# A transformer block on one core: the products of P and V of a head pair in four groups instead of six

## The reference, cut to what matters

```python
# x: (2, 1024, 512) f32, 16 heads of d = 32
h = layernorm(x)
Q, K, V = (h @ Wq.T + bq), (h @ Wk.T + bk), (h @ Wv.T + bv)     # each cut into 16 heads
Q, K = rope(Q), rope(K)
scores = einsum('bhqd,bhkd->bhqk', Q, K) / sqrt(32)
attn = softmax(where(causal, scores, -inf), axis=-1)
x = x + einsum('bhqk,bhkd->bhqd', attn, V).reshape(...) @ Wo.T + bo
g, u = (layernorm(x) @ gate_w.T) * gate_s, (layernorm(x) @ up_w.T) * up_s
x = x + ((silu(g) * u) @ down_w.T) * down_s
```

## Time and profile before

| what | value |
|---|---|
| time, median of 3 runs | 858.93 us (858.11 to 862.7) |
| the profiled execution | 860.51 us, its span 858.5 us |
| PE busy | 779.1 us (91%) |
| DVE busy | 476.4 us (55%) |
| ACT busy | 329.0 us (38%) |
| POOL busy | 247.7 us (29%) |
| share of the chain that ended last | PE 66%, DVE 9%, DMA 8%, issue 8%, SP's queue 4%, ACT 3% |
| the products of P and V, L1106 | 768 records, 144.7 us busy |

### The profile page before, as it was taken

The page is one execution under the profiler, slowest core; times in us unless marked ns, Lnnn a source line. Parts: engine busy times, 40 slices in busy tenths (PEclk is TensorE's granted clock), DMA queues, the critical chain, the costliest instruction groups (busy, mean ns, idle before and its releaser), DMA issues.

```text
span 858.5 us, 10688 instructions
## 1 busy us (share of the span) xinstructions
PE 779.1 (91%) x3520; PEld 537.8 (63%) x3520; DVE 476.4 (55%) x1102; ACT 329.0 (38%) x669; POOL 247.7 (29%) x224
## 2 busy tenths in 40 slices
PE   4899999977999999999999999946999999999996
PEld 3678787744444445454444444735788888888885
DVE  5877596976667666767676744527412413314112
ACT  3423333424555555555555555210223223223221
POOL 0514152501113131313131315715122322323223
PEclk9989999967999999999999999986999999999999
DMA  8085634854556565656565626760000100100001
GB/s 269 29 325 192 220 122 172 262 181 126 137 138 163 138 164 139 163 138 162 138 162 139 163 65 196 269 286 1 1 0 1 50 1 0 49 1 24 27 0 51
DMA packets 52012, 104.37 MB, mean 122 GB/s; under 512 B 14820, under 2 KB 15332, under 8 KB 51444
## 3 DMA queue, kind: packets, MB, share of 16 engines
q1 hardware_dynamic: 51960, 103.72, 38.9%
HBM read 69.62 MB, written 38.21 MB: 126 GB/s over the span
## 4 chain that ended last, share of the span: by engine, by line
PE 66%; DVE 9%; DMA 8%; issue 8%; SPq 4%; ACT 3%; POOL 2%; DVEq 0%; ACTq 0%; POOLq 0%
PE ps L1002 31%; PE ps L1106 11%; PE ps L1180 9%; PE ps L1066 8%; PE ps L1087 5%; DMA flag_st<-in_ffn 5%; SPq L389 2%; DVE masked L855 2%; PE ps L994 2%; DMA qk_scratch<-st_lo 1%; DVE neg_max L873 1%; POOL xr L532 1%; ACT xT_hi L566 1%; DVE w_lo L768 1%; DVE rot L799 1%
## 5 line engine op out<-in xcount | busy, mean ns | idle before, releaser
L647 ACT ACTIVATE p<-ps 128x384 f32<-128x384 f32 (+3 forms) x384 | 171.9, 492 | 160.7 <-PE ps L1087 157.4
L1066 PE MATMUL ps<-k_st,q_st 96*128 96x512 f32 (+2 forms) x384 | 147.9, 411 | 21.8 <-DVE row_max L855 14.0
L855 DVE CUSTOM_DVE_ANT_0 masked<-ps,mask_qk 128x256 bf16<-128x256 f32 (+3 forms) x256 | 120.6, 500 | 66.5 <-PE ps L1066 65.8
L1106 PE MATMUL ps<-p,v_slot 128*64 128x512 f32 (+3 forms) x768 | 144.7, 500 | 1.2 <-ACT o_raw L654 1.2
L1066 PEld LDWEIGHTS ps<-k_st,q_st 96*128 96x128 f32 x384 | 72.6, 197 | 103.7 <-issue 51.9
L1087 PE MATMUL ps<-q_st,k_st 99*128 99x384 f32 (+2 forms) x384 | 131.3, 362 | 5.4 <-DMA q_st<-neg_max_T 4.0
L961 DVE SCALAR_TENSOR_TENSOR hid<-ps,us_sb,silu 128x512 f32<-128x512 f32 x44 | 33.0, 750 | 169.0 <-PE ps L1002 166.5
L516 POOL TENSOR_SCALAR_AFFINE_SELECT p<-p 128x512 f32<-128x512 f32 x64 | 41.0, 640 | 253.6 <-ACT p L647 253.6
L551 POOL TENSOR_TENSOR hid_lo<-hid,hid_hi 128x512 fp32r<-128x512 f32 x44 | 56.8, 1292 | 180.1 <-ACT hid_hi L722 180.1
L1106 PEld LDWEIGHTS ps<-p,v_slot 128*64 128x64 f32 x768 | 46.1, 136 | 66.9 <-issue 57.3
L857 DVE TENSOR_REDUCE row_max<-ps 128x1 f32<-128x512 f32 (+1 forms) x128 | 83.1, 651 | 4.4 <-PE ps L1066 2.0
(11 more groups left out here) (94 smaller groups left out, 1118.2 us busy)
## 6 DMA issues: line engine op xcount, KB each, us to landing
qk_scratch<-st_hi SPq DMA_DIRECT2D x32, 512.0 KB, 3.9
q_st<-qk_scratch SPq DMA_DIRECT2D x32, 384.0 KB, 4.2
k_st<-qk_scratch SPq DMA_DIRECT2D x32, 384.0 KB, 5.0
flag_st<-in_ffn SPq DMA_DIRECT2D x32, 264.0 KB, 2.8
ffn_copy<-in_ffn SPq DMA_DIRECT2D x32, 264.0 KB, 3.2
qk_scratch<-st_lo SPq DMA_DIRECT2D x16, 512.0 KB, 4.3
o_T<-o_raw SPq DMA_DIRECT2D x32, 128.0 KB, 2.6
rec_l<-rec_rows SPq DMA_DIRECT2D x32, 128.0 KB, 3.3
```

The costliest lines, as they stand in the source:

```text
L647: act.activation(p32[:, at:at + q0 + w - keep], ps[:, ST_BANK + i % RING, keep - q0:w], ACT.Exp, scale=SCALE).then_inc(exp_done, 1)
L855: ins = dve.tensor_tensor_reduce(masked[:, s_before(i) % 2, col:col + kept], scores, mask_qk[:, 512 - kept:512], 1.0, NEG, ALU.add, ALU.ma ...
L1066: ins = pe.matmul(ps[:, S_BANK + i % RING, col:col + w], q_st[0:K_DOT, slot, qt * P:(qt + 1) * P], k_st[0:K_DOT, slot, k0:k0 + w], start=T ...
L1106: ins = pe.matmul(ps[VW * a:VW * (a + 1), O_BANK + half, q0 - 512 * half:512], v_slot[:, slot, kt, :], p32[:, at:at + n], start=(kt == 0), ...
```

## The change

The pair's twelve (half, kt) are cut in four groups in place of six, and a step issues two groups, at its places 3 and 9, in place of three at 3, 7 and 11. The products themselves are the same.

```diff
-PV_AFTER = (3, 7, 11)
-PV_GROUPS = [[(0, 0), (0, 1)], [(0, 2), (0, 3), (1, 0)], [(1, 1), (1, 7)],
-             [(1, 2), (1, 6)], [(1, 3)], [(1, 4), (1, 5)]]
+PV_AFTER = (3, 9)
+PV_GROUPS = [[(0, 0), (0, 1), (0, 2), (0, 3)], [(1, 0), (1, 1)], [(1, 2), (1, 3), (1, 7)], [(1, 4), (1, 5), (1, 6)]]
...
                     if t >= 2 and i in PV_AFTER:
-                        output_products(t // 2 - 1, 3 * (t % 2) + PV_AFTER.index(i))
+                        output_products(t // 2 - 1, len(PV_AFTER) * (t % 2) + PV_AFTER.index(i))
```

## The result

The changed kernel takes 889.5 us in the median (four runs, 887.71 to 891.02), the kernel before 860.73 beside it (four runs, 858.11 to 862.7). The ratio is 1.0335, with an interval of 1.0295 to 1.0376: slower by 3.4%. The forecast was 871, with a range from 862 to 877. The sign was right, the size was not.

What follows compares the result with a forecast made beforehand. Bound: a loop from PE's transposition over SP's issues and the weights' piece to DVE's test. Steady part +9.4, steps 2 and 3 +0.9, 28 to 30 +0.1, t = 31 +1.6: +12.0 us, median about 871, range 862 to 877.

Steps and rivals of the forecast that it cites:

- The bound: Stage B's steady part: steps end on a loop through PE's transposition and DVE's test, not on PE's work alone.
- the loop: Stage B: PE's transposition, ACT's copy, SP's DMA issues, weights' piece, DVE's test, next step's first matmul; slack about 0.1 us.
- Longer group ahead of the transposition: Place 3 of each step: 384 more columns cost 0.64 us a step, with bounds 0.5 to 0.64.
- Fewer groups: Stage B: one group less a step gains nothing behind the transposition; 0.35 us a step if that cover were gone.
- POOL and the test: Odd steps: POOL's mask no longer lies over DVE's test, 0.33 us off each, bounds 0 and 0.33.
- Steps in which POOL scales: Four or five steps of B: the longer group hides under an existing wait; no loss, a gain of 0.1 at most.
- The end of B: Step t = 31: more products stand ahead of the last exponential, +1.6 us, bounds 0.6 to 1.9.
- Steps 28 to 30: Behind B's steady part: t = 28 costs 0; in 29 and 30 the saved 0.35 meets new waits; +0.1 us.
- The clock: Stage B: the sum adds nothing for a falling granted clock, as PE would idle only 1 us of 11.
- the third rival: Stage B: clock falls to 1.2 GHz in one step of ten, some 25 us on top, 896; chance 0.05.

Runs made afterwards that it cites:

- e1: The changed kernel, but SP issues the load of the weights' piece and its copy ahead of the two DMAs with the maxima; 829.58 us, ratio 0.9625.
- e2: The kernel before, six groups, with SP's load of the weights' piece and its copy issued ahead of the maxima's DMAs; 838.82 us, ratio 0.9746.
- e3: The kernel before, six groups at places 3, 7 and 11, but the first group as long as the changed kernel's; 880.72 us, ratio 1.0221.
- e5: The changed kernel, four groups at its two places, but each step's first group as short as before (896 and 768 columns); 858.04 us, ratio 0.9978.
- e11: e1 with the last group of B put back to place 11 in the last step; 825.73 us, ratio 0.9636.
- e4: The changed kernel with each step's last scores bank issued five times, about 1 us more PE work a step; 876.27 us, ratio 1.0182.
- e10: The changed kernel with each step's last scores bank issued twice, 0.24 us more PE work a step; 878.42 us, ratio 1.0233.
- e8: The kernel before, PE's program untouched, but SP issues the piece's copy in DRAM ahead of the load for DVE's test; 901.24 us, ratio 1.0478.
- e7: The order of e1, but one group of products a step, at place 7 behind the transposition (two groups a pair); 893.39 us, ratio 1.0403.
- e9: e1 with POOL's scaling in every fourth step moved between its two masks; 837.06 us, ratio 0.9745.

## Why the prediction was wrong in size and right in sign

**The bound.** Right. The wait in SP's order was named as the loop, and e1 and e2 cut it: the steady part falls from 284.9 to 236.3 us with four groups, and from 257.3 to 246.0 with six.

**Longer group ahead of the transposition.** Right, at the full clock. The first products took 2.37 us (2.36 foretold) and 2.16 (2.15), the transposition stands 4.90 after the step in even steps, the test begins 4.9 to 5.5 us behind it (5.1 foretold), the next start has PE idle for the maxima in all steps, 32.2 us in total where "over 20" was foretold. The even step at the full clock is 11.14 to 11.32 (11.20 foretold), the odd one 10.91 (10.89). e3 and e5 show that this length, and not the number of groups, is the cause.

**Fewer groups.** Right that they gain nothing under the loop (e5). The price if the cover is gone was given as 0.35 us a group; e1 against e2 measured 0.48 in the plain steps and 0.40 over all. The Trainium skill (TensorEngine Tiling (Array Packing), Key Properties) says that a change of the tiling drains TensorE. With PE as the bound the runs fit this, but none of them separates such a drain from other costs of a group; the 0.48 us is the price of the group as a whole.

**POOL and the test.** Right. All 24 tests of the steady part take 0.71 us. (The top of the forecast's range, 877, stands for this term, but 871 + 4.6 is 875.6; nothing hangs on it.) In e3, where the place 7 remains, the mask still lies over about half of them.

**Steps in which POOL scales.** Right: the steps t = 8, 12, 16, 20 and 24 take 11.14 to 11.32, as the others do.

**The end of B.** The term was sized 1.6, with bounds to 1.9; it measured 2.1 in the change, and 1.96 in e11 against e1. Steps 28 to 30, put at 0.1, cost 3.1, of which 2.3 are t = 28 (13.72 us against 11.46), in which the clock fell.

**The clock: the step that failed.** The sum put the granted clock at nothing, and the third rival ("If it fell to 1.2 GHz in one step out of ten") was given a chance of 0.05, because "in the new steps PE would be idle 1 us of 11, not 4 of 10". The idle time came out somewhat longer than foretold, 0.95 to 1.62 us and 1.3 in the mean, where 0.5 to 1.2 stood. That it leaves the clock alone was an inference from two stretches far apart, 0.6 us of 10.6 and 4 of 10. The clock fell in 10 of the 24 steps. The trace of the kernel before had a case in between, which was overlooked, step t = 2 at the start of B:

```profile
205.72:218.55 12.83, 12.53 (x53) 6.76 (x54) 7.27 (x25) 5.96 (x14) 1.17 (x2) 0.80 0.31 91
```

PE had idled 2.83 us ahead of it, the mean clock was 0.80, and the step took 12.83 us, where such steps take 10.5 at the full clock: a price of 2.3 us for a fall. The rival's price was mis-sized in the other direction: such a step costs 1.8 us more, not 8.8, since the low clock lasts for a part of the step only. That the rival's own figure, 896, lies near the measured 889.5 is luck: it counts too few falls at too high a price.

The low clock hits mostly the products at place 3, which take 3.6 to 4.1 us instead of 2.15 in eight of the nine odd steps with a fall (2.61 in t = 27). They stand ahead of the transposition, so the loop passes them on, and PE idles again at the next start. Whether the same fall would cost less behind the transposition, no run here shows. 10 x 1.76 = 17.6 us is what the forecast lacks, and 12.0 + 17.6 = 29.6 of the 30.5. That this comes so close is in part luck: outside the steady part the forecast had 2.6 us and the measured sum is 3.0, but its parts are off by up to 3 us and cancel. e4 and e10 show the cause by its opposite: more work for PE, less time. e8 shows it without any change to PE's work.

The Trainium skill (TensorE: Matmul & The Clock Gate, A second HAM failure mode: psum-queue depth-cycling) tells of a kernel whose PE idles briefly between groups of matmuls so often that its clock goes back and forth. The trace agrees, with a fall in ten steps of 24. Weighed beside the rows, that section would have been a reason to give the rival more than 0.05.

**What stays open.** What decides in which step the clock falls. In the steady parts it never fell behind 0.9 us of idle time or less (before, e4, e5, the plain steps of e7). In the changed kernel it fell in nine of the ten steps that began with 1.38 us or more, and in one of the 14 that began with 1.25 or less. But t = 25 kept it with 1.56, in e8 a step kept it with 1.70, and in e9 the same 1.53 us were followed by a fall twice and by none twice. So the length of the idle time makes a fall likely and does not settle it, and no run here says what does. A kernel with the change's loop and its idle time taken away in some steps only was not tried.

## What to carry to other kernels

Before costing a longer or shorter group, find what is issued behind it in the other queues: here a transfer that needs nothing from the maxima stood behind them in SP's order, and it decided whether the change gained 9 us or lost 29. Cut such a loop first, then look at the change again. Where a change gives PE idle time that returns every step, count the clock as a cost, not only the idle time; if it falls, the work in the microseconds behind the idle time is what gets slower, and if that work is ahead of a loop, the loop is longer by it.

## What the runs showed of the hardware

- The granted clock fell in 10 of 24 steps that began with 1.0 to 1.6 us of PE's idle time (1.2 to 1.6 in the ten), and 1 us of useless matmuls a step brought the kernel from 889.5 to 876.3 us.
- In the ten steps the fall came 0.3 to 2.2 us after PE had started again, and it lasted some 3.4 us (once 6.9), with PE busy all the time. In step t = 2 of the kernel before, where PE idled 2.83 us, the low clock was there when PE started.
- The same 1152 columns of products: 2.15 us at the upper level, 3.6 to 4.1 at place 3 of eight of the nine odd steps with a fall.
- A group of products on the array's two halves between other matmuls costs 0.48 us beside its columns (10.10 against 9.63 us a step), where the chain of waits before the change had given 0.35.
- POOL's work over DVE: the test of 528 columns takes 0.71 us alone, 1.0 to 1.2 under a mask of 0.64, and 2.71 under a scaling of 2.36; a negation of 8 columns takes 2.18 under the same, and 0.17 alone (e1). The Trainium skill (SBUF — State Buffer, Who interferes with whom) says of a DVE instruction with two SBUF inputs that it contends with a GpSimd instruction that reads SBUF; for the test the runs agree.
